# Another order of work in the opening of a state-space and expert-mixture kernel

## What is computed

```python
# first block, on x = layernorm(input)
x = lin(x, w1)
x = silu(depthwise_conv(x, conv_w, conv_b))      # 3 taps along the rows
x_delta = softplus(lin(x, dl_w, dl_b))
A_bar = exp(-x_delta * lin(x, A_w, A_b))
A_cum = cumprod(A_bar, axis=1)
h = cumsum(lin(x, B_w, B_b) * A_cum, axis=1)
ssm = lin(h, C_w, C_b) + lin(x, D_w, D_b)
out = ssm + lin(ssm * silu(lin(ssm, w2)), w3)
# second block, on xn = layernorm(...) * gamma + beta
out = sum over the chosen experts: comb[:, e] * swiglu(xn, gate_up_w[e], down_w[e])
out = out + swiglu(xn, shared_gate_up_w, shared_down_w)
```

## Time and profile before

| | us |
|---|---|
| median of 3 runs | 1140.29 |
| lowest and highest of them | 1137.35 and 1142.83 |
| the profiled execution | 1128.52 |
| its span in the trace | 1126.8 |
| mean granted TensorE clock | 0.976 of full |

### The profile page before, as it was taken

The page is one execution under the profiler, slowest core; times in us unless marked ns, Lnnn a source line. Parts: engine busy times, 40 slices in busy tenths (PEclk is TensorE's granted clock), DMA queues, the critical chain, the costliest instruction groups (busy, mean ns, idle before and its releaser), DMA issues.

```text
span 1126.8 us, 22452 instructions
## 1 busy us (share of the span) xinstructions
PE 1030.6 (91%) x7042; PEld 908.7 (81%) x7042; DVE 802.1 (71%) x2056; ACT 624.0 (55%) x1269; POOL 285.0 (25%) x302
## 2 busy tenths in 40 slices
PE   3889999989989999899999999999999999999940
PEld 2666777677667565799999999999999899999940
DVE  5986899898978857766666666666666566666645
ACT  6767868776775455345454444444544444444415
POOL 1133123542352263212121211212111112112125
PEclk9999999999999999999999999999999999999975
DMA  8655666874675587964653521855357822368149
GB/s 299 228 208 190 231 212 225 280 268 172 208 246 200 173 281 273 366 235 136 196 171 100 185 38 23 254 146 140 86 194 227 276 33 33 89 190 257 30 102 215
DMA packets 123563, 208.96 MB, mean 185 GB/s; under 512 B 9840, under 2 KB 75120, under 8 KB 123504
## 3 DMA queue, kind: packets, MB, share of 16 engines
q1 hardware_dynamic: 108096, 188.33, 48.9%
q0 software_dynamic: 15408, 19.93, 10.1%
HBM read 357.61 MB, written 85.50 MB: 393 GB/s over the span
## 4 chain that ended last, share of the span: by engine, by line
PE 67%; DVE 10%; SPq 7%; issue 5%; DMA 4%; POOL 3%; ACT 2%; another core or an unknown queue 1%; DVEq 0%; ACTq 0%; POOLq 0%
PE bank L479 10%; PE bank L1447 8%; PE bank L1449 8%; PE bank L1448 8%; PE bank L1492 4%; PE bank L1494 4%; PE bank L1493 4%; PE bank L473 4%; PE bank L474 3%; PE bank L475 3%; DMA w_both<-w_split 2%; POOL xs_scratch L1213 2%; SPq L1314 2%; PE bank L1465 1%; PE bank L1463 1%
## 5 line engine op out<-in xcount | busy, mean ns | idle before, releaser
L1396 POOL DMA_INDIRECT acc_scratch<-cv,ids x71 | 111.4, 1568 | 514.7 <-DVE cv L1592 491.4
L1629 DVE TENSOR_SCALAR cv<-bank 128x256 f32<-128x256 f32 x284 | 120.5, 424 | 160.7 <-PE bank L1449 135.8
L1559 ACT ACTIVATE cv<-cv 128x256 f32<-128x256 f32 x284 | 118.7, 418 | 184.4 <-DVE cv L1629 181.5
L1447 PE MATMUL bank<-h_hi,w_both 128*128 128x256 f32 x744 | 208.2, 280 | 5.7 <-DMA w_both<-w_split 4.5
L1448 PE MATMUL bank<-h_hi,w_both 128*128 128x256 f32 x744 | 206.2, 277 | 0.0
L1449 PE MATMUL bank<-h_hi,w_both 128*128 128x256 f32 x744 | 206.1, 277 | 0.0
L1545 ACT ACTIVATE h_lo<-cv 128x256 fp32r<-128x256 f32 x248 | 103.3, 417 | 88.4 <-DVE cv L1632 86.9
L1632 DVE TENSOR_TENSOR cv<-bank,cv 128x256 f32<-128x256 f32 x284 | 120.3, 424 | 41.1 <-ACT cv L1559 38.8
L1447 PEld LDWEIGHTS bank<-h_hi,w_both 128*128 128x128 f32 x744 | 140.0, 188 | 8.8 <-issue 4.4
L1448 PEld LDWEIGHTS bank<-h_hi,w_both 128*128 128x128 f32 x744 | 139.8, 188 | 0.0
L1449 PEld LDWEIGHTS bank<-h_hi,w_both 128*128 128x128 f32 x744 | 139.8, 188 | 0.0
(11 more groups left out here) (273 smaller groups left out, 2643.9 us busy)
## 6 DMA issues: line engine op xcount, KB each, us to landing
w_both<-w_split SPq DMA_DIRECT2D x180, 512.0 KB
single_ring<-w_split SPq DMA_DIRECT2D x18, 3840.0 KB
w_both<-w_split SPq DMA_DIRECT2D x180, 256.0 KB
single_ring<-w_split SPq DMA_DIRECT2D x18, 1536.0 KB
e_raw<-w_e SPq DMA_DIRECT2D x64, 384.0 KB
w_split<-e_high SPq DMA_DIRECT2D x64, 384.0 KB
w_split<-e_raw SPq DMA_DIRECT2D x64, 384.0 KB
xs_hi<-w_split SPq DMA_DIRECT2D x30, 512.0 KB
```

Source lines behind the costliest of these rows:

```text
L1447: nc.tensor.matmul(out, gu_hi[f][:, cols], xg_hi[:, par, c, :], start=c == 0, stop=False)
L1559: nc.scalar.activation(gate[:, f % 4, :], gate[:, f % 4, :], ACT.Silu).then_inc(silu_ready, 1)
L1629: nc.vector.tensor_scalar(half, gate_ps, CLIP, -CLIP, ALU.min, ALU.max).then_inc(clipped, 1)
```

## The change

Only the order of work changes, in two places. In SyncE's opening the loads of the first two expert chunks move from the end of the list to behind the load of the B weights, and so ahead of C, D, w2, w3, the router and the shared expert. In the ORDER table the opening of batch 0 is rewritten on ScalarE and VectorE, and one stage moves on GpSimd; TensorE's and SyncE's words stay as they are. The core of the diff:

```diff
             "scalar":
-                "p0/0 N0/0 N1/0 t0/0 t1/0 t2/0 p1/0 t3/0 p2/0 u0/0 w0/0 w1/0 u1/0 u2/0 u3/0 c0/0 c1/0 p3/0 w2/0 S0/0 S1/0 r0/0 r1/0 "
-                "c2/0 c3/0 w3/0 p4/0 S2/0 be0/0 S3/0 exp0/0 ln0/0 be1/0 exp1/0 ln1/0 r2/0 r3/0 abar0/0 w4/0 be2/0 exp2/0 be3/0 "
...
+                "N0/0 N1/0 t0/0 t1/0 t2/0 t3/0 p0/0 u0/0 w0/0 u1/0 p1/0 u2/0 c0/0 u3/0 c1/0 S0/0 r0/0 S1/0 r1/0 c2/0 w1/0 c3/0 p2/0 "
+                "S2/0 be0/0 S3/0 w2/0 exp0/0 ln0/0 be1/0 exp1/0 ln1/0 r2/0 r3/0 abar0/0 w3/0 p3/0 be2/0 exp2/0 be3/0 abar1/0 exp3/0 "
...
             "vector":
-                "m0/0 m1/0 k/0 p0/0 p1/0 w0/0 p2/0 w1/0 c0/0 c1/0 p3/0 w2/0 r0/0 r1/0 c2/0 c3/0 m0/1 w3/0 dt0/0 p4/0 da0/0 dt1/0 "
...
+                "m0/0 m1/0 k/0 p0/0 w0/0 p1/0 c0/0 c1/0 r0/0 r1/0 c2/0 w1/0 c3/0 p2/0 w2/0 dt0/0 da0/0 dt1/0 r2/0 da1/0 ac0/0 bx0/0 "
...
             "gpsimd":
-                "m0/0 m1/0 m0/1 lo0/0 lo1/0 lo2/0 lo3/0 tab/0 lo4/0 m1/1 lo5/0 d0.5/0 lo6/0 lo7/0 d0.6/0 d1.5/0 d1.6/0 lo0/1 lo1/1 "
+                "m0/0 m1/0 lo0/0 lo1/0 lo2/0 lo3/0 tab/0 m0/1 lo4/0 m1/1 lo5/0 d0.5/0 lo6/0 lo7/0 d0.6/0 d1.5/0 d1.6/0 lo0/1 lo1/1 "
...
-            for n in range(2, len(weights)):
+            load_weights(raw_w, *weights[2], w_raw_loaded[2])
+            for n in range(WS - 1):
+                load_raw(n)
+            for n in range(3, len(weights)):
                 load_weights(raw_w, *weights[n], w_raw_loaded[n])
...
-            for n in range(WS - 1):
-                load_raw(n)
```

## The result

| | before | change |
|---|---|---|
| median of 20 runs each, us | 1136.84 | 1141.08 |
| lowest and highest | 1131.66 and 1142.83 | 1135.21 and 1146.10 |
| ratio of change to before, 95% interval | | 1.0037 (1.0023 to 1.0051) |
| the profiled execution | 1128.52 | 1140.71 |
| its span | 1126.8 | 1139.0 |

The change is 4.2 us slower, inside the 0.5% that I had called no change, and its time is within 0.2 us of the 1140.9 forecast. Part of that closeness is luck: the kernel before has a median of 1136.84 over 20 runs, 3.5 under the 1140.29 of the first three from which I counted. Against it I had forecast +0.6, and +4.2 came; what happened inside is further from the forecast than the total, as the part on the prediction shows.

A forecast was written before the change was run, and what follows sets the result against it. TensorE was taken as the bound behind the opening, VectorE's list between TensorE's two opening waits. The 1.8 us head start is spent catching up chunks and 0.6 more: 1140.3 + 0.6 = 1140.9 us, range 1131 to 1148.

The forecast's parts named there:

- Step 1: Opening: rows normalised before the dl weights are copied; TensorE starts at 10.15 not 11.09, u finished 0.95 us sooner.
- Step 2: First convolution: with less work in front, TensorE starts on the first xs_lo at 24.55 not 28.99, 4.4 us sooner.
- Step 3: At 62 us: 1.8 of the 4.4 us remain, so the delta TensorE waits for comes at 60.2; bounds 0.7 to 4.4.
- which I put at 0.6: VectorE before 62 us: cost of splitting C's weights where it does not wait, 0.6 us off the head start.
- what two chunks fewer bring: VectorE's list up to 62 us: two expert chunks fewer, 2 x 0.87 = 1.74 us sooner.
- Step 4: Front of batch 1: postponed chunks catch up, chunk 17 loads late; the 1.8 us head start is spent and 0.6 more.
- what TensorE feels of it: Batch 1: late chunk 17 reaches TensorE through ScalarE's d1.6/0 and e0/0; y1/0 starts at 131.85, 1.0 us later.
- A: The forecast: the gain is made and spent at chunk 17; 1138.8 to 1143.3 us, chance 0.52.
- C: Slower: stores landing 1.1 us later each delay chunks 16 to 19, ScalarE stands repeatedly; 1142.3 to 1144.5 us, chance 0.19.
- B: The head start survives, early loads hiding their fixed cost; 1138.5 us, at best 1134.7, chance 0.22.
- D: Opening makes no head start (first L473 later than 26) but catching up still costs; 1142.5 us, chance 0.07.
- Costed at nothing: ScalarE's 2 us wait at chunk 13, C, D and shared weights landing some 2 us later, GpSimd's later m0/1: 0.

The follow-up runs named there:

- norm_only: Kernel before with only the row normalising and three of four transposed-row copies put ahead of the dl weights on ScalarE; ratio to before 0.9984, repeated 0.9974.
- p3_gap: The change with the low part of C's weights moved in front of bx0 on VectorE in batch 0; ratio to before 1.0031.
- lag_only: Kernel before, opening and loads unchanged, with expert chunks two places behind through batch 0 and caught up at the front of batch 1; ratio to before 1.0025.
- open_nolag: The change's opening and early loads, but chunks back at before's pace from the first h, some weight splits behind the first delta; ratio to before 0.9987.
- before_again: The kernel before, unchanged, profiled a second time; one execution at 1134.38 us.
- loads_only: Kernel before with only the first two expert chunk loads moved ahead of C, D and the shared weights; ratio to before 1.0003.
- norm_lag1: Kernel norm_only with one chunk postponed from in front of the first xs_lo and caught up at 75 to 80 us; ratio to before 0.9977.
- w1_later: The change with chunks 16 and 17 moved further back on ScalarE and VectorE at the front of batch 1; ratio to before 1.0046.

## Why the prediction was right or wrong

**Step 1, normalising first: right in place, its worth too small.** TensorE starts at 10.15 as forecast. u ends at 21.8, 0.8 later than the 20.95 that I said: I had kept the 6.88 us of the earlier trace rows for the product by w1, and it took 7.65. Against four profiles with the dl weights first, not one, the sooner start is worth 1.65 us and not 0.95, and norm_only shows a gain of 2 to 3 us that lasts to the end.

**Step 2, the first convolution: nearly right.** A wait of 3.86 (3.6 forecast), the first L473 at 25.62 (24.55), half clock behind it as in the kernel before: 3.4 us of the 4.4 came. The missing 1.0 is mostly the longer product by w1.

**Step 3, what is left at 62 us: failed.** I forecast 60.2 and got 63.76: 1.8 sooner was 1.7 later. I had counted VectorE's work on both sides of the convolution as though the rest of the row would move with it. Three terms were wrong. The largest is p3, "which I put at 0.6", with an upper bound of 1.13: it cost 2.2 by p3_gap, 1.3 in VectorE's list and 0.9 since it pushed the decay for which TensorE waited and the lower clock came behind that wait. The second is the 0.7 us by which VectorE was to be ahead behind the convolution. The delta of unit 0 hangs on the convolution's fourth side and then on ScalarE's row of silu, chunk and table load; TensorE's wait of 2.66 for it has its own half clock behind it; and with the first L473 3.4 us sooner, bx0 is at 41.83, as in the kernel before (41.85 there): 0.7 became nothing. The third is what two chunks fewer bring, 1.74 in my sum: lag_only shows 0.7 for it. In place of 0.7 + 1.74 - 0.6 = 1.8 sooner the runs show 0 + 0.7 - 2.2, that is 1.5 later, of the 1.7 measured. Part of a new opening without the debt does no better: open_nolag has dl7 at 62.71, norm_only at 61.81.

Against before_again, whose first load landed later, the change is level at dl7 (63.76 and 63.53) and 0.6 ahead at 84 us. What it never has is the 1.8 that I carried on.

**Step 4, the chunks catch up: right up to be0/1, then the path to TensorE wrong.** Counted from dl7, the load of chunk 17 was forecast for 58.1 us later and came 57.9 later (121.65), be0/1 for 63.2 and came at 62.9 (126.61); without the full clock behind dl7 both would have been some 0.8 later. ScalarE's wait for chunk 17, 3.16, is near the 3.8 forecast, with one of 1.63 for chunk 16 in front of it that I did not have. What failed is "what TensorE feels of it": 1.0 us at y1/0, by way of ScalarE's d1.6/0 and e0/0. I had followed the late chunk on ScalarE alone. VectorE stands for it in order as well (3.23), with times1/0 behind it, and TensorE waits 3.77 us for that in front of 128.43, at half clock behind it; y1/0 starts at 137.23, not 131.85. lag_only measures the price of catching up as 5.2 and the change as 5.5 over the 55.15 of before, where my sum had 1.8 + 0.6 = 2.4.

So dl4/1, at 144.77 for 139.0, is 5.8 late: 3.6 from step 3, 3.1 from the price of catching up, and 0.8 given back by full clock behind dl7, which no step had. That the time still fell into the range of A is the luck named with the result.

**The rivals.** C decided "from the point where chunk 16 is loaded later than 114.6"; it was loaded at 116.65, ScalarE stood for two chunks in turn, and the loss lies at C's upper end (2.0 to 4.2 over before; 4.2 came). So C is nearer to what came about, though I gave it 0.19 and A 0.52. Not all of it came: chunks 18 and 19 did not make ScalarE stand again, and the reason that I gave, stores that land 1.1 us late each, did not decide. The store in front of chunk 17's load took 3.70 (117.95 to 121.65) where I had 3.2. Nor was it the lost head start: p3_gap is 1.0 ahead of before at 84 us and pays 5.7. B fell. Its rule from the Trainium skill, page "DMA: Bandwidth & Descriptors", section "Rules for kernel authors", to issue early and wait late, holds for chunk 0 here and is worth nothing by loads_only (1.0003); at chunks 16 and 17 the issue itself waits for a slot. D fell: the first L473 came at 25.62.

**Costed at nothing.** The 2 us that I saw coming at chunk 13 were 0.34, and hidden: from 84 us to the start behind the wait for s (107.05 before, 107.94 in the change) both kernels take 23.79. The later loads of C, D and the shared weights cost nothing (loads_only).

**What stays open.** What decides which level of the clock is granted behind a wait of about 2 us. Why the product by w1 takes 7.07 us in one execution and 8.28 in another. How the 4.9 us at dl4/1 (against before_again) become 4.2 by the end in one comparison and 6.5 in the other (1.0058) is not settled; batch 3 differs between two executions of the same kernel by as much. Why norm_lag1 gives half of a chunk was not followed up.

## What to carry to other kernels

A step postponed is a debt: look up, in the trace, where the stream that feeds it (here loads that wait for stores) has slack, and pay it back there. Two chunks caught up at the front of batch 1 cost 4.2 to 5.7 us at dl4/1; one caught up at 75 to 80 us cost nothing there. And follow a wait for such a stream on every engine that touches it, not on one. Before counting a head start, follow it through every engine to the next place where all wait for one another; a start 3.4 us sooner was used up 16 us later at bx0. And of a change that does several things, run the smallest part: reordering two steps of ScalarE's opening gained 2 to 3 us, the whole rewrite lost 4. Before reading an interval as a price, split it where the clock can differ: from dl7 the debt seemed to cost 4.0, from 84 us on it cost 5.2.

## What the runs showed of the hardware

The price of a wait of TensorE is not its length alone: a stretch at the lower of the clock's two levels (0.5 of full, 1.2 GHz) can come behind it, and the length of the wait does not settle whether it does. Behind the wait in front of the first L473, 3.86 to 7.37 us, it came in every profile. Behind 2.48 us it came in the change and behind 2.49 us it did not in w1_later, with the same order of work before it. Behind dl7's wait of 2.15 to 2.20 us it came in eight profiles and did not in six. In open_nolag it is absent behind 1.22 and present behind 1.92:

```profile
34.90:37.00 2.10, 1.72 (x7) 1.12 (x7) 1.50 (x2) 2.07 (x4) 0.59 (x2) 1.00 0.48 192
43.30:45.00 1.70, 1.67 (x5) 1.34 (x6) 1.70 (x2) 1.70 (x4) 0.00 (x0) 0.64 0.67 213
```

Where the profiles give pairs (behind decay and behind dl7), such a stretch cost 0.8 to 1.2 us. It comes and goes between executions of kernels with the same order, so a part of their scatter is this, and a single profile can't price a wait of about 2 us.

The landing of one and the same first load differs between executions by over a microsecond, 7.99 and 9.32 for the dl weights, and what is put in front of everything else should not depend on it.
